# Six-layer attention and feed-forward on one core: values products behind the scores, feed-forward input by DMA, two groups normalised early

## What is computed

```
x = attn_layer(shift_tokens(x)) + x
x = ffn_layer(shift_tokens(x)) + x

shift_tokens(t): features 0..63 stay; features 64..127 come from the token before (zeros for token 0)
attn_layer: q, k, v = split(x @ Wqkv)              # 16 heads of 64
            q, k = l2norm, scaled, rotated
            window of 32 queries sees 64 keys; softmax; @ v; @ Wo
ffn_layer:  xn = layer norm of x
            a, gate = split(xn @ W1 + b1)          # 341 columns each
            a * gelu(gate) @ W2 + b2
```

## Time and profile before

| | us |
|---|---|
| median of 3 runs | 2305.26 |
| lowest and highest of them | 2302.34, 2305.34 |
| the profiled execution's own time | 2298.88 |
| its span | 2297.1 |

### The profile page before, as it was taken

How to read it: one execution, slowest core, us unless ns; L and a number is a source line. 1 busy time by engine, 2 the same in 40 slices (tenths; PEclk the granted TensorE clock), 3 DMA queues, 4 the chain that set the end, 5 groups by cost and what they waited for, 6 DMA issues and landing times.

```text
span 2297.1 us, 104869 instructions
## 1 busy us (share of the span) xinstructions
PE 2163.7 (94%) x36357; PEld 1677.6 (73%) x36357; DVE 1708.3 (74%) x4617; ACT 1555.0 (68%) x5192; POOL 1410.4 (61%) x2639
## 2 busy tenths in 40 slices
PE   6999789998999989999899998999989999899998
PEld 4776267776888758887588875788857888578885
DVE  4777878886888758787578875778757877578874
ACT  3553545554888748887488884888848888478883
POOL 3442711112888728887288882888828888288881
PEclk9997999997999999999999999999999999999999
DMA  3000000001211102111021110311103111021110
GB/s 102 0 0 1 0 1 0 0 0 54 75 41 42 35 26 75 40 42 35 23 77 42 41 36 18 81 42 39 39 18 79 42 40 40 16 51 43 42 40 20
DMA packets 120016, 82.33 MB, mean 36 GB/s; under 512 B 50998, under 2 KB 112580, under 8 KB 119876
## 3 DMA queue, kind: packets, MB, share of 16 engines
q1 hardware_dynamic: 119876, 80.43, 13.5%
HBM read 21.94 MB, written 1.05 MB: 10 GB/s over the span
## 4 chain that ended last, share of the span: by engine, by line
PE 74%; issue 5%; DVE 4%; POOL 2%; ACT 1%; DVEq 0%; POOLq 0%; ACTq 0%
PE bank L818 14%; PE bank L835 9%; PE bank L902 7%; PE bank L882 6%; PE bank L862 6%; PE bank L827 6%; PE bank L892 4%; PE bank L845 4%; PE bank L757 2%; PE bank L854 2%; PE bank L746 2%; PE bank L949 2%; PE bank L948 2%; PE bank L605 2%; PE bank L959 1%
## 5 line engine op out<-in xcount | busy, mean ns | idle before, releaser
L534 POOL TENSOR_TENSOR l_qk<-l_rot 128x512 f32<-128x512 f32 x384 | 494.2, 1287 | 106.0 <-DVE l_rot L1597 58.8
L1593 DVE TENSOR_TENSOR l_rot<-bank,l_tab 128x512 f32<-128x512 f32 x384 | 265.0, 690 | 185.7 <-ACT l_sq L1194 185.1
L1210 ACT ACTIVATE l_qkT<-bank 128x512 f32<-128x512 f32 x384 | 229.6, 598 | 255.2 <-PE bank L835 255.2
L555 POOL TENSOR_TENSOR l_qk<-l_qk,l_rn 128x512 f32<-128x512 f32 x384 | 400.7, 1044 | 0.9
L1174 ACT ACTIVATE prob<-bank,peak 128x64 f32<-128x64 f32 x1536 | 353.9, 321 | 1.3 <-DVE peak L1615 1.3
L818 PE MATMUL bank<-w_high,xs_part 128*128 128x512 f32 x768 | 347.4, 452 | 6.0 <-DVE xs_part L1584 5.4
L1597 DVE TENSOR_TENSOR l_rot<-bank,l_tab 128x512 f32<-128x512 f32 x384 | 261.4, 681 | 0.0
L1607 DVE TENSOR_REDUCE l_ss<-l_sq 128x8 f32<-128x512 f32 x384 | 259.6, 676 | 0.2
L835 PE MATMUL bank<-const,l_qk 128*128 128x128 f32 x1536 | 252.9, 287 | 6.5 <-POOL l_qk L555 5.8
L1194 ACT ACTIVATE l_sq<-bank 128x512 f32<-128x512 f32 x384 | 236.0, 615 | 23.8 <-PE bank L818 16.0
L902 PE MATMUL bank<-l_wo,l_oT 128*128 128x128 f32 x1536 | 237.4, 277 | 0.0
(11 more groups left out here) (201 smaller groups left out, 5287.8 us busy)
## 6 DMA issues: line engine op xcount, KB each, us to landing
...
```

What stands on the lines that cost most here:

```text
L534: pool.tensor_tensor(l_qk[:, k], l_rot[:, k, 0], l_rot[:, k, 1], ALU.add).then_inc(l["add_done"], 1)
L555: pool.tensor_tensor(v, v, l_rn[:, k, :, None].broadcast_to([128, 8, L_DIM]), ALU.mult).then_inc(l["qk_done"], 1)
L1593: dve.tensor_tensor(l_rot[:, k, 0].rearrange("p (q h n) -> p q h n", q=2, h=4), bank[:, 0, :].rearrange("p (q h n) -> p q h n", q=2, h=4), ...
```

## The change

- PE: the transposes of q and k stand ahead of the scores, so that the values products follow the scores directly.
- POOL: scaling is first in the slot, and the Newton step is last and one slot earlier (skew 3). The step has three instructions instead of four; the square of the guess is now made by ACT (new stage `l_square_guess`, skew 3, behind the copy of x).
- DVE: the rotation stands ahead of the residual.
- SP: the shifted half of x comes by two DMAs, of 112 rows and of 15 rows, instead of one of 127.
- Feed-forward input: `f_shift` is gone. `take_feed_forward` brings each group's shifted input from Y into f_x by three DMAs (128, 112 and 15 rows of four sequences), for groups 0 and 1 after the loop, for group 2 behind sequence 13's values, for group 3 at the end. DVE takes statistics and normalises from there.
- Statistics, rstd and norm of groups 0 and 1 run in the attention's last slots, with two buffers each; the transposed groups use banks 1 and 2 in turn.
- Semaphores of the earlier stages' norms are shared under new names (`ln`, `ln2`), with counts that go on; that part is left out below.

```diff
         f_b1 = sb("f_b1", [128, 2, len(CHUNKS)])
         f_b2 = sb("f_b2", [128, D])
         f_st = sb("f_st", [128, 4, 6])
-        f_mv = sb("f_mv", [128, 4, 2])
-        f_rs = sb("f_rs", [128, 4])
-        f_n = sb("f_n", [128, 4, D])
+        f_mv = sb("f_mv", [128, 2, 4, 2])
+        f_rs = sb("f_rs", [128, 2, 4])
+        f_n0 = sb("f_n", [128, 4, D])
+        f_n = (f_n0[:], c_oT[:, 1])
+        f_x = m_xT[:]
         f_nT = sb("f_nT", [128, 2, 512])
         f_ge = sb("f_ge", [128, 2, 512])
...
+        def feed_forward_read(eng, ly, g):
+            late = g // 3
+            eng.wait_ge(ld_fx[late], (ly + 1) * (48 if late else 144))
+        SHIFTED = slice(0, 112), slice(112, S - 1)
         def one(t3, b):
...
                 sp.dma_start(xin[:, k, 0:HALF], x[:, 0:HALF]).then_inc(ld_xin[k], 16)
-                sp.dma_start(xin[1:, k, HALF:], x[0:S - 1, HALF:]).then_inc(ld_xin[k], 16)
+                for rows in SHIFTED:
+                    sp.dma_start(xin[rows.start + 1:rows.stop + 1, k, HALF:], x[rows, HALF:]).then_inc(ld_xin[k], 16)
             def next_x(ly, b, k):
                 sp.wait_ge(l["x_turned"], upto(ly * B, b + 1))
                 apart(sp)
                 take_x(ly, b + 2, k)
+            def take_feed_forward(ly, first, end):
+                sp.wait_ge(l["res_done"], upto(ly * B, end))
+                apart(sp)
+                for b in range(first, end, 4):
+                    four = slice(b, b + 4)
+                    sp.dma_start(f_x[:, four, 0:HALF], Y[:, four, 0:HALF]).then_inc(ld_fx[b // 12], 16)
+                    for rows in SHIFTED:
+                        sp.dma_start(f_x[rows.start + 1:rows.stop + 1, four, HALF:], Y[rows, four, HALF:])\
+                          .then_inc(ld_fx[b // 12], 16)
             def serve_layer(ly, last):
...
                                 apart(sp)
                             load_projections(ly + 1, 2 * b + q)
                 load_feed_forward(ly)
-                with sp.Fori(2, B // 2 - 1) as i:
+                with sp.Fori(2, B // 2 - 2) as i:
                     for k in range(2):
                         move_values(ly, 2 * i + k, k, 0)
                         next_x(ly, 2 * i + k, k)
                         move_values(ly, 2 * i + k, k, 1)
-                for b in range(B - 2, B):
+                take_feed_forward(ly, 0, 8)
+                for b in range(B - 4, B):
                     for q in range(2):
                         move_values(ly, b, b % 2, q)
+                        if q == 0 and b < B - 2:
+                            next_x(ly, b, b % 2)
+                    if b == B - 3:
+                        take_feed_forward(ly, 8, 12)
+                take_feed_forward(ly, 12, 16)
...
...
                     k = j % 2
                     y, t = l_y[:, k], l_t[:]
-                    pool.wait_ge(l["guessed"], upto(ub, u + 1))
-                    pool.tensor_tensor(t, l_s[:, k], y, ALU.mult).then_inc(l["newton"], 1)
-                    pool.wait_ge(l["newton"], upto(3 * ub, 3 * u + 1))
-                    pool.tensor_tensor(t, t, y, ALU.mult).then_inc(l["newton"], 1)
-                    pool.wait_ge(l["newton"], upto(3 * ub, 3 * u + 2))
+                    pool.wait_ge(l["squared"], upto(ub, u + 1))
+                    pool.tensor_tensor(t, l_s[:, k], l_yy[:, k], ALU.mult).then_inc(l["newton"], 1)
+                    pool.wait_ge(l["newton"], upto(2 * ub, 2 * u + 1))
                     apart(pool)
                     pool.tensor_scalar(t, t, -0.5, 1.5, ALU.mult, ALU.add).then_inc(l["newton"], 1)
-                    pool.wait_ge(l["newton"], upto(3 * ub, 3 * u + 3))
+                    pool.wait_ge(l["newton"], upto(2 * ub, 2 * u + 2))
                     pool.tensor_tensor(l_rn[:, k], t, y, ALU.mult).then_inc(l["rn_done"], 1)
...
-                return Pipeline(pool, [(4, l_norm), (3, l_add), (4, l_scale)], UNITS, UNROLL, 4)
-            def feed_forward(ly, *groups):
+                return Pipeline(pool, [(4, l_scale), (3, l_add), (3, l_norm)], UNITS, UNROLL, 4)
+            def feed_forward(ly):
                 fb = ly * 4
-                for g in groups:
-                    yg = Y[:, 4 * g:4 * g + 4, :]
+                def f_rstd(g):
+                    rs = f_rs[:, g % 2]
                     pool.wait_ge(f["stat"], upto(0, fb + g + 1))
                     apart(pool)
-                    pool.tensor_scalar(f_rs[:], f_mv[:, :, 1], LN_EPS, None, ALU.add).then_inc(f["pool_st"], 1)
+                    pool.tensor_scalar(rs, f_mv[:, g % 2, :, 1], LN_EPS, None, ALU.add).then_inc(f["pool_st"], 1)
                     pool.wait_ge(f["pool_st"], upto(0, fb + g + 1))
-                    pool.tensor_tensor(f_rs[:], f_rs[:], minus_half[:, 0:4], ALU.pow).then_inc(f["rstd"], 1)
-                    pool.wait_ge(f["xs"], upto(0, fb + g + 1))
+                    pool.tensor_tensor(rs, rs, minus_half[:, 0:4], ALU.pow).then_inc(f["rstd"], 1)
+                def f_bias(g):
+                    yg = Y[:, 4 * g:4 * g + 4, :]
+                    feed_forward_read(pool, ly, g)
                     pool.tensor_tensor(yg, yg, f_b2[:, None, :].broadcast_to([128, 4, D]),
                                        ALU.add).then_inc(f["yb_done"], 1)
+                return f_rstd, f_bias
             def into_feed_forward(ly, att):
+                rstd_n, bias = feed_forward(ly)
                 att.steady()
-                att.finish(0, 1, 2, 3)
+                att.finish(0)
+                rstd_n(0)
+                att.finish(1)
+                rstd_n(1)
+                att.finish(2, 3)
                 pool.wait_ge(ld_fw, (ly + 1) * (16 * FW_DMAS))
-                feed_forward(ly, 0)
+                bias(0)
             def out_of_feed_forward(ly, nxt):
-                feed_forward(ly, 1, 2, 3)
+                rstd_n, bias = feed_forward(ly)
+                rstd_n(2)
+                bias(1)
+                rstd_n(3)
+                bias(2)
+                bias(3)
                 if nxt is not None:
                     nxt.start(*range(UNROLL))
...
-                stages = [(5, l_scores), (4, l_turn_qk), (6, l_pv), (1, l_project_qk), (1, l_project_v), (7, l_output), (6, l_turn_o), (5, l_turn), (0, l_turn_x)]
+                stages = [(4, l_turn_qk), (5, l_scores), (6, l_pv), (1, l_project_qk), (1, l_project_v), (7, l_output),
+                          (6, l_turn_o), (5, l_turn), (0, l_turn_x)]
                 return Pipeline(pe, stages, UNITS, UNROLL, 4)
             def feed_forward(ly):
                 fb, ub = ly * 4, ly * UNITS
-                def f_shift(g):
-                    v = bank[:, 1, :].rearrange("p (a n) -> p a n", a=4)
-                    yg = Y[:, 4 * g:4 * g + 4, :]
-                    pe.wait_ge(l["res_done"], upto(0, ly * B + 4 * g + 4))
-                    if g == 0:
-                        pe.wait_ge(l["v_done"], upto(ub, UNITS))
-                    else:
-                        pe.wait_ge(f["n_done"], upto(0, fb + g))
-                    pe.matmul(v[:, :, 0:HALF], ident, yg[:, :, 0:HALF], start=True, stop=True)
-                    pe.matmul(v[:, :, HALF:], shift_t, yg[:, :, HALF:], start=True, stop=True).then_inc(f["xs"], 1)
                 def f_turn(g):
                     pe.wait_ge(f["n_done"], upto(0, fb + g + 1))
                     if g == 0:
+                        pe.wait_ge(l["v_done"], upto(ub, UNITS))
+                    if g == 1:
                         pe.wait_ge(l["qkT_done"], upto(ub, UNITS))
-                    pe.wait_ge(f["nT_done"], upto(0, fb + g))
+                    pe.wait_ge(f["nT_done"], upto(0, fb + g - (g > 0)))
                     for n in range(4):
-                        ins = pe.transpose(bank[:, 2, n * 128:(n + 1) * 128], f_n[:, n], ident)
+                        ins = pe.transpose(bank[:, 1 + g % 2, n * 128:(n + 1) * 128], f_n[g % 2][:, n], ident)
                     ins.then_inc(f["turned"], 1)
...
...
                                             f_w2[0:n, k, :], start=k == 0, stop=k == len(CHUNKS) - 1)
                     ins.then_inc(f["out_mm"], 1)
-                return f_shift, f_turn, f_hidden, f_out
+                return f_turn, f_hidden, f_out
             def into_feed_forward(ly, att):
-                shift, turn_n, hidden, _ = feed_forward(ly)
+                turn_n, hidden, _ = feed_forward(ly)
                 att.steady()
-                att.finish(0, 1)
-                shift(0)
-                att.finish(2, 3)
+                att.finish(0, 1, 2)
+                turn_n(0)
+                att.finish(3)
+                turn_n(1)
                 pe.wait_ge(ld_fw, (ly + 1) * (16 * FW_DMAS))
-                turn_n(0)
                 att.finish(4)
                 hidden(0, 0)
-                att.finish(5)
-                shift(1)
-                att.finish(6)
+                att.finish(5, 6)
                 hidden(0, 1)
             def out_of_feed_forward(ly, nxt):
```

(51 more changed lines are left out.)

78 lines of the change are left out of this document (42 added, 36 removed).

## The result

Median of four runs each: 2338.4 us (2333.4 to 2341.1) after, 2303.8 (2298.9 to 2305.3) before, ratio 1.0154 with a 95% interval of 1.0132 to 1.0176. The profiled execution took 2341.1 (span 2339.2, before 2297.1). The forecast said 2257 and 0.86 for faster, so sign and size are wrong; the 2338 lies beside the rival called "slower" (2331).

What follows compares the result with a forecast made beforehand. TensorE, busy 94% of the span, was taken as the bound. Slots -55, first slots -3 and tail with feed-forward +10 summed to -48 us, 2257 predicted; 8 in 10 range 2214 to 2291.

Steps and rivals of the forecast that it cites:

- slower: Rival: POOL's queue holds the scaling behind the statistics twice a layer in the tail; 2331 us with no slot gain, chance 0.09.
- Order of PE's slot: Attention slot on TensorE: with transposes first and both packed groups together, PE alone would run at 3.33 us, saving 0.26.
- passages: TensorE's slot: each switch between full-array and packed work costs about 0.1 to 0.15 us, four a slot.
- x: TensorE's slot: the time between the scores and the values products once adjacent, taken as 0.02 us.
- Who keeps up: Attention slot: softmax wait ends 0.05 us late, queue work shows; slot 3.43 us, saving 0.16 (bounds 0.26 and 0.02).
- the term for the queue: Before the values products: TensorE's queue working through their waits puts 0.07 us a slot on the path, between 0 and 0.21.
- a rival of 0.14: Values products starve: x is 0.14 or all 0.21 of queue work shows; slot gains 0.03 to 0.11, 2288 us, chance 0.14.
- POOL and ACT: Attention slot: POOL needs 3.2 us and ACT 3.26 a slot, both covered by PE by 0.1 to 0.2.
- Tail: Attention's last slots: scaling waits behind DVE's statistics, PE stands 5 us, then again for group two; +6.9 us a layer.
- Feed-forward: Feed-forward up to the next layer's L818: three shifts and the 2.50 stand go, 2.2 comes back; together -6.1 us a layer.
- Transfers: SP's queue: the added DMAs, about 0.65 us each, are covered; nothing counted.

## Why the prediction was wrong, step by step

*Order of PE's slot.* The passages were right: transposes in 0.44, and x is nothing but a step (0.267 from scores to values products when only one wait stands between, against the 0.27 taken). The Trainium skill (TensorEngine Tiling (Array Packing), Key Properties) says that a change of tiling mode drains TensorE, and that different tiles can load weights and multiply in parallel. The 0.267 agrees: where the mode stays, no passage shows. Of the prediction's four passages the rows measure three; the one into the scores was never seen apart from the masks. What failed is a later sentence, that "inside a group 8 ns is all that stands between products". That holds behind full-array work only. Behind another packed group the 32 take 0.27 (the change) to 0.40 (waits moved ahead), not 0.19, from first to last weight load, in the mean.

*Who keeps up.* The softmax was not late: the wait for copied probabilities is 10.0 us in all, 6.5 before, and none of it lies in the 56 slots. The step that failed is the term for the queue: "I take 0.07, a third". By the mean steps, the 0.66 for both groups became 0.86, so list and pace together cost 0.20, close to the upper end 0.21 that I had made a rival of 0.14. With most of the list gone 0.81 was left, so 0.15 of it is the pace of 64 products in a row, which the prediction had at nothing, and about 0.05 the list, which it had named. With the smaller steps lost around the slot's head, 0.02 to 0.03 was left of the slot's 0.16. The slots came to -10 for -55, half of the 90 us between the forecast's -48 and the span's +42. I had written the lower bound, 0.02, beside the term. It is what came, but by another cause than the list, so that is in part luck.

*POOL and ACT.* Both were covered, as said: no wait for them shows in the 56 slots, and undoing TensorE's order alone with every loop written out leaves the slot (3.646) within 0.01 of the kernel before with its loops written out (3.651).

*Tail.* The mechanism was right at each step: L884 started at +6.86, forecast +7.0; the second time 7.76 later, forecast 6.9. Mis-sized by 1.4 a layer, +9.2 for the forecast's +6.9 and +0.9 for its clock, since the slot between the two stands ran at 1.2 GHz. Taking the cause away took 6.8 of the 9.2.

*Feed-forward.* This step failed: "Together -6.1". It gave 0.9 in the mean: 2.8 in layer 0, which has no jump ahead of it, 0.2 in layers 1 and 2, a loss of 0.5 in layer 3 and 1.6 in layer 4. Taking away the stand of 2.50 before L932 I wrote that 2.2 would come back from VectorE, and never asked what else lay beneath it. The jump did, with 3.4 us in two layers, 1.6 and 2.1 in two others, and half clock behind it (PEclk 0.90, before 0.95). Behind the jump lay the gating, behind the gating ACT's two stands, and all three covers had to go before a gain showed. A norm from SBUF beside POOL was a cost that I had not considered. With all covers gone the stretch is 30.2, 4.4 under before and 3.8 under the kernel before with its loops written out; -6.1 was too much even so.

*The rivals.* "Slower" had the right mechanism and the right point: it decides once a slot gains under 0.08, and a slot gained 0.02 to 0.03. That its 2331 lies so near is partly luck: it had nothing for the slots, where 10 us came, and 21 us back from the feed-forward, where 4 came. I gave it 0.09 because I held the slot's gain to be safe. Yet the other terms were a loss in sum, so the 0.86 for faster rested on that one number, whose lower bound was below the deciding point.

*Transfers.* Nothing waited for a feed-forward DMA: the largest idle time in front of L1698 is 0.3. The split into 112 and 15 rows was not tried by itself.
